# Second MLP in 128-token tiles that go by way of memory, with the inverse transform at a chunk's head and a new order of root, rows, bias row and transpositions

## The reference

```
h = layernorm(x, g1, be1)
h = afno2d(h, w1, b1, w2, b2)       # rfft2, block-diagonal filter, irfft2, + h
h = h + residual                     # called x3 here
m = layernorm(h, g2, be2)
m = gelu(m @ fc1_w + fc1_b) @ fc2_w + fc2_b
return m + h
```

## Time and profile before

| | us |
|---|---|
| median of 3 runs | 1118.7 (1117.19 to 1119.45) |
| profiled execution, own time | 1113.01 |
| its span (all times below count from its start) | 1111.2 |
| second MLP with its first inverse transform: 1012.56 to the end | 98.6 |
| second MLP, start of `up(0)` to the last matmul | 1022.53 to 1107.14 |

### The profile page before, as it was taken

One profiled execution on the slowest core, in us unless ns is written; L12 is line 12 of the kernel. 1 busy time (PEld: TensorE's weight loads), 2 busy tenths in 40 slices (PEclk: granted clock), 3 DMA queues, 4 the chain that ended last, 5 costly groups with the idle time before them and its releaser, 6 DMA issues.

```text
span 1111.2 us, 35967 instructions
## 1 busy us (share of the span) xinstructions
PE 1033.5 (93%) x15606; PEld 731.5 (66%) x15606; DVE 847.2 (76%) x1714; ACT 700.6 (63%) x1003; POOL 170.7 (15%) x142
## 2 busy tenths in 40 slices
PE   5867889999999999999999999999989889998998
PEld 3545246665777776677776767676657776775776
DVE  4837978889999999999999999999526764233443
ACT  4646157677787777777777877777865442231554
POOL 4430000910000000000000000000024544001443
PEclk9885579999999999999999999999999999999999
DMA  4698967657474756565656566554400001211110
GB/s 122 172 223 271 239 119 167 107 99 129 85 121 93 111 97 107 96 107 101 103 100 105 104 99 108 96 95 88 80 13 21 25 23 34 68 54 41 40 45 23
DMA packets 83011, 109.17 MB, mean 98 GB/s; under 512 B 14109, under 2 KB 75234, under 8 KB 82661
## 3 DMA queue, kind: packets, MB, share of 16 engines
q1 hardware_dynamic: 82853, 106.87, 48.9%
HBM read 85.40 MB, written 21.44 MB: 96 GB/s over the span
## 4 chain that ended last, share of the span: by engine, by line
PE 71%; DVE 12%; DMA 7%; ACT 5%; issue 3%; POOL 2%; SPq 0%; DVEq 0%; ACTq 0%; POOLq 0%
PE ps L1028 35%; PE ps L1189 17%; PE ps L1023 15%; DVE mx_p L1485 4%; DVE xh L101 2%; POOL rstd L109 1%; DMA m_d<-mneg 1%; DVE stage_lo L1454 1%; PE ps L1041 1%; ACT hid_f L955 1%; DVE stats L88 1%; DMA rel_d<-stage_lo 1%; DMA rel<-in_c_rel_w 1%; PE ps L1135 1%; DMA qv<-m_d 1%
## 5 line engine op out<-in xcount | busy, mean ns | idle before, releaser
L1485 DVE TENSOR_REDUCE mx_p<-ps 128x1 f32<-128x464 f32 (+1 forms) x1080 | 608.6, 629 | 34.4 <-PE ps L1028 23.2
L905 ACT ACTIVATE prob<-ps 128x768 f32<-128x768 f32 x648 | 496.2, 810 | 184.9 <-PE ps L1028 184.1
L1028 PE MATMUL ps<-kc,qc 112*32 112x464 f16 (+1 forms) x4320 | 460.4, 370 | 8.6 <-issue 4.4
L1028 PE MATMUL ps<-qv,ka 113*32 113x384 f16 x5184 | 403.8, 328 | 10.3 <-DMA qv<-m_d 7.7
L1189 PE MATMUL ps<-prob,v_ext 128*32 128x384 f32 x2592 | 293.3, 487 | 2.5 <-issue 2.0
L1028 PEld LDWEIGHTS ps<-qv,ka 113*32 113x32 f16 x5184 | 213.9, 97 | 86.7 <-issue 28.6
L1028 PEld LDWEIGHTS ps<-kc,qc 112*32 112x32 f16 x4320 | 173.2, 95 | 108.0 <-DVE mx_p L1485 30.0
L1189 PEld LDWEIGHTS ps<-prob,v_ext 128*32 128x32 f32 x2592 | 117.0, 111 | 17.4 <-issue 3.2
L1023 PE MATMUL ps<-w_dn,hid 128*96 128x192 f16 x864 | 77.5, 249 | 6.6 <-DVE hid L1540 4.4
L1023 PEld LDWEIGHTS ps<-w_dn,hid 128*96 128x96 f16 x864 | 73.2, 125 | 12.0 <-issue 6.1
L752 POOL COPY v_ext<-v_all 128x288 f32<-128x288 f32 x12 | 5.1, 427 | 480.6 <-PE ps L1189 480.5
(11 more groups left out here) (106 smaller groups left out, 838.2 us busy)
## 6 DMA issues: line engine op xcount, KB each, us to landing
qv<-rel_d SPq DMA_DIRECT2D x216, 144.0 KB
qv<-kq_d SPq DMA_DIRECT2D x108, 216.0 KB
qc<-rel_d SPq DMA_DIRECT2D x24, 216.0 KB, 4.0
xin<-in_x SPq DMA_DIRECT2D x12, 288.0 KB, 3.3
kq_d<-khl SPq DMA_DIRECT2D x24, 144.0 KB, 2.3
q_h<-kq_d SPq DMA_DIRECT2D x9, 288.0 KB, 4.7
q_w<-qw_d SPq DMA_DIRECT2D x9, 288.0 KB, 6.7
rel_d<-stage_hi SPq DMA_DIRECT2D x4, 648.0 KB, 7.6
```

What stands on the lines that cost most here:

```text
L905: nc.scalar.activation(prob[:, s4(p, s), :].rearrange("p (a b) -> p a b", a=2), ps[:, 3 + 2 * (s % 2):5 + 2 * (s % 2), 0:CW], ACT.Exp).the ...
L1028: ins = nc.tensor.matmul(ps[c:c + 32, bank, 0:w], l[:, c:c + 32], r, start=True, stop=True, tile_position=(0, c))
L1485: nc.vector.tensor_reduce(mx_p[:, q * GT + k // MP, k % MP:k % MP + 1], ps[:, slot, 0:min(MW, N - k % MP * MW)], AX, ALU.max).then_inc(uni ...
```

## The change

1. `down` of the second MLP works on 128-token tiles (W = 128): three tiles a chunk, 54 matmuls instead of 72, each with a stationary operand of 128 columns instead of 96.
2. The sum then needs x3 with 128 tokens on 128 partitions. SP writes x3 of a chunk to `x3_d` in memory and reads it back as `x3t` (128 x 3 x 192, two buffers); the sum (now two instructions) writes `y_o`, which is stored. `rows` is loaded on 128 partitions.
3. The row fc2_b is added to `x3t` by POOL (`bias_into_wide`, 576 elements a partition) at the head of a chunk; `bias_into` of x3 is gone from the second MLP.
4. PE does `inverse_w(c+1)` at the head of the chunk, ahead of `up(c)`, and the transpositions after the hi products of tiles 0 and 2 and ahead of their lo products.
5. POOL takes the root after hidden slices 0 and 1 and does slices 2 and 3 behind it. DVE does its hidden slices 4 and 5 behind the normalized rows, not beside the root, and the next input's lo part behind them.

```diff
+            def to_wide_tiles(c):
+                rows_c = x3_d[c * CW:(c + 1) * CW, :]
+                sp.wait_ge(x3_ok, c + 1)
+                sp.dma_start(rows_c.rearrange("(t p) c -> p t c", p=T), x1[:, ds(c * CT, CT), :]).then_inc(x3_out, 16)
+                sp.wait_ge(x3_out, 16 * (c + 1))
+                sp.dma_start(x3t[:, c % 2, :, :], rows_c.rearrange("(j p) c -> p j c", p=128))\
+                  .then_inc(x3t_in[c % 2], 16)
...
             def block1(c, more):
                 if more:
                     load_u2(c + 1)
                 if not is_at(c, 0):
                     store_out(c - 1)
+                if more:
+                    to_wide_tiles(c + 1)
 
             load_u2(0)
+            to_wide_tiles(0)
...
+            def bias_into_wide(c):
+                pool.wait_ge(x3t_in[c % 2], 16 * (c // 2 + 1))
+                x = x3t[:, c % 2, :, :]
+                nc.gpsimd.tensor_tensor(x, x, rows[:, 3:4, :].to_broadcast([128, 3, C]), ALU.add).then_inc(x3b_ok, 1)
+
             def block1(c, more):
-                lo_of_hidden(c, up1, range(POOL_TILES))
+                bias_into_wide(c)
+                lo_of_hidden(c, up1, range(2))
                 if more:
                     norm_root(pool, nc, rstd, ln4, c + 1)
-                    bias_into(c + 1, 3, ln4, x3b_ok)
+                lo_of_hidden(c, up1, range(2, POOL_TILES))
...
             def down(c, i, sems, half_way):
+                W, late = (T, (1, 3)) if i == 0 else (128, (1,))
...
+                if i == 1:
+                    half_way()
                 pe.wait_ge(sems["lo"], (c + 1) * HM)
                 for t in (0, 2):
                     lo_products(t)
-                half_way()
-                for t in (1, 3):
+                if i == 0:
+                    half_way()
+                for t in late:
...
             def block1(c, more):
-                up(c, 1, up1, {2: lambda: inverse_w(c + 1)} if more else {})
+                if more:
+                    inverse_w(c + 1)
+                up(c, 1, up1, {})
                 down(c, 1, up1, lambda: norm_transposed(c + 1, ln4, t4_ps) if more else None)
...
                 norm_chunk(dve, nc, x3_c, stats, mv, rstd, xh2[0], ln4, c,
                            lambda: wait_used(dve, t4_ps, c), beside_root)
-                lo_of_input(c, 1)
 
             def block1(c, more):
                 tiles = range(POOL_TILES, HM)
                 if more:
-                    inverse(c + 1, lambda: lo_of_hidden(c, up1, tiles))
-                else:
-                    lo_of_hidden(c, up1, tiles)
-                mlp_sum(c, up1, x3b_ok, lambda: wait_used(dve, y_out, 16 * c))
+                    inverse(c + 1, lambda: None)
+                lo_of_hidden(c, up1, tiles)
+                if more:
+                    lo_of_input(c + 1, 1)
+                dve.wait_ge(up1["dn_ps"], c + 1)
+                dve.wait_ge(x3b_ok, c + 1)
+                wait_used(dve, y_out, 16 * c)
...
+                nc.vector.scalar_tensor_tensor(out=y[:, 0:2 * C], in0=ps[:, 2, 0:2 * C], scalar=1 / WS,
+                                               in1=x3[:, 0:2 * C], op0=ALU.mult, op1=ALU.add)
+                nc.vector.scalar_tensor_tensor(out=y[:, 2 * C:3 * C], in0=ps[:, 3, 0:C], scalar=1 / WS,
+                                               in1=x3[:, 2 * C:3 * C], op0=ALU.mult, op1=ALU.add)\
+                  .then_inc(up1["sum"], 1)
```

More of the change, by code:

```diff
@@ L129, in build @@
         u1_d = nc.dram_tensor("u1_d", (S, 2, KF, C), F32).ap()
+        x3_d = nc.dram_tensor("x3_d", (N, C), F32).ap()
         u2_d = nc.dram_tensor("u2_d", (S, 2, KF, C), F32).ap()
@@ L134, in build @@
             khl = sb("khl", [C2, 2, 4, 2, CW], F16, r)
+        with ExitStack() as r:
+            x3t = sb("x3t", [128, 2, 3, C], F32, r)
+            y_o = sb("y_o", [128, 3, C], F32, r)
         attn = sb("attn", [T, NT, C])
@@ L143, in build @@
         shift = [sb(f"shift{i}", [C2, 2]) for i in range(3)]
-        rows = sb("rows", [T, 4, C])
+        rows = sb("rows", [128, 4, C])
         ident = sb("ident", [128, 128])
@@ L312, in build @@
         x3b_ok = sem("x3b_ok")
+        x3_out = sem("x3_out")
+        x3t_in = [sem("x3t_in0"), sem("x3t_in1")]
         ln4 = norm_sems("ln4")
@@ L319, in build @@
         x_t = d["x"].rearrange("(t p) c -> p t c", p=T)
-        out_t = out.rearrange("(t p) c -> p t c", p=T)
         NCONST = [0]
@@ L338, in load_weights @@
             for i, nm in enumerate(("L0_conv_mlp_b2", "L1_conv_g1", "L1_conv_be1", "L1_conv_fc2_b")):
-                load(eng, rows[:, i, :], d[nm].rearrange("(o c) -> o c", o=1).to_broadcast([T, C]))
+                load(eng, rows[:, i, :], d[nm].rearrange("(o c) -> o c", o=1).to_broadcast([128, C]))
         def load_transforms(eng):
@@ L695, in store_out @@
                 sp.wait_ge(up1["sum"], c + 1)
-                sp.dma_start(out_t[:, ds(c * CT, CT), :], y_sb[:, :, :]).then_inc(y_out, 16)
+                sp.dma_start(out[c * CW:(c + 1) * CW, :].rearrange("(j p) c -> p j c", p=128), y_o[:, :, :])\
+                  .then_inc(y_out, 16)
+            def to_wide_tiles(c):
[5 more added lines that the diff above has]
+                  .then_inc(x3t_in[c % 2], 16)
             def block1(c, more):
@@ L785, in bias_into @@
                 x1_c = x1[:, ds(c * CT, CT), :]
-                nc.gpsimd.tensor_tensor(x1_c, x1_c, rows[:, row:row + 1, :].to_broadcast([T, CT, C]),
+                nc.gpsimd.tensor_tensor(x1_c, x1_c, rows[0:T, row:row + 1, :].to_broadcast([T, CT, C]),
                                         ALU.add).then_inc(done, 1)
@@ L1277, in hi_products @@
                         for part in range(2):
-                            mm(down_tile(t), hid[:, m, 0, t * T:(t + 1) * T], w_dn[i][:, part, m, :],
+                            mm(down_tile(t), hid[:, m, 0, t * W:(t + 1) * W], w_dn[i][:, part, m, :],
                                start=(m == 0 and part == 0), stop=False)
@@ L1282, in lo_products @@
                     for m in range(HM):
-                        ins = mm(down_tile(t), hid[:, m, 1, t * T:(t + 1) * T], w_dn[i][:, 0, m, :],
+                        ins = mm(down_tile(t), hid[:, m, 1, t * W:(t + 1) * W], w_dn[i][:, 0, m, :],
                                  start=False, stop=(m == HM - 1))
@@ L1287, in down_tile @@
                 def down_tile(t):
-                    return ps[0:T, 2 + t // 2, (t % 2) * C:(t % 2 + 1) * C]
+                    return ps[0:W, 2 + t // 2, (t % 2) * C:(t % 2 + 1) * C]
                 wait_used(pe, sems["sum"], c)
@@ L1557, in block0 @@
                 nc.vector.tensor_tensor(h1[:, :, :], xh2[1][:, :, :],
-                                        rows[:, 1:2, :].to_broadcast([T, CT, C]), ALU.mult).then_inc(h1_mul, 1)
+                                        rows[0:T, 1:2, :].to_broadcast([T, CT, C]), ALU.mult).then_inc(h1_mul, 1)
                 dve.wait_ge(h1_mul, c + 1)
                 nc.vector.tensor_tensor(h1[:, :, :], h1[:, :, :],
-                                        rows[:, 2:3, :].to_broadcast([T, CT, C]), ALU.add).then_inc(h1_ok, 1)
+                                        rows[0:T, 2:3, :].to_broadcast([T, CT, C]), ALU.add).then_inc(h1_ok, 1)
             chunks(block0)
@@ L1596, in block1 @@
                 if more:
-                    inverse(c + 1, lambda: lo_of_hidden(c, up1, tiles))
-                else:
-                    lo_of_hidden(c, up1, tiles)
-                mlp_sum(c, up1, x3b_ok, lambda: wait_used(dve, y_out, 16 * c))
+                    inverse(c + 1, lambda: None)
[5 more added lines that the diff above has]
+                wait_used(dve, y_out, 16 * c)
+                x3 = x3t[:, c % 2, :, :].rearrange("p t c -> p (t c)")
+                y = y_o[:, :, :].rearrange("p t c -> p (t c)")
+                nc.vector.scalar_tensor_tensor(out=y[:, 0:2 * C], in0=ps[:, 2, 0:2 * C], scalar=1 / WS,
[3 more added lines that the diff above has]
+                  .then_inc(up1["sum"], 1)
             inverse(0, lambda: None)
+            lo_of_input(0, 1)
             chunks(block1)
```

1 line of the change is left out of this document (removed).

## The result

The changed kernel takes 1128.9 us (median of 4 runs, 1127.7 to 1132.8) against 1118.0 for the kernel before in the same comparison: ratio 1.012, 95% interval [1.0086, 1.0155]. That is 11 us slower, and outside the range of the prediction (1115.5 to 1123.1). The profiled execution took 1128.54 us with a span of 1126.8.

A forecast was written before the change was run, and what follows sets the result against it. PE was taken to bound a chunk, but for ACT's gelus. Five chunks at +0.61 (+3.05), last chunk -1.49, last sum -0.1 and chunk 0 -0.3 gave +1.2 us: 1119.9 us, 78%, range 1115.5 to 1123.1.

The forecast's parts named there:

- The pitch of the wide matmuls: PE in `down`: matmuls with 128-column stationary operands keep 82.5 ns each, so 18 fewer save 1.49 us a chunk.
- rival (c): PE in `down`: wide weight loads set the pitch, 98 ns, +3.2 us on top, 1123.1 us; chance 8%.
- The hole before slice 2: PE in `up`: without the inverse transform there, the wait for ACT's gelu of slice 0 is bare, +0.58 in five chunks.
- The last chunk: Second MLP's last chunk: no rows and no bias row, so the full saving of 1.49 us.
- rival (b): `x3t` lands only after 11.4 us of a chunk, so rows end at 10.4; chunk 13.9, 1114.6 us; chance 7%.
- rival (a): DVE and POOL don't hold each other up: rows end at 9.25 us, chunk 13.25, 1111.4 us; chance 7%.
- the bias row ends: POOL: bias row of the next chunk, 1.36 us behind hidden slices 2 and 3, ends 11.1 us into a chunk.
- The -0.3 at chunk 0's head: Chunk 0: the inverse transform may fill some of PE's 0.89 us idle; -0.3 us, bounds -0.9 and +1.0.
- Step 1: DVE's four rows beside POOL: one passes after each POOL instruction, the last goes free; rows end at 11.5 us.
- Step 2: PE before the transpositions: idle of 1.4 us a chunk, priced at its own length, with no clock term.
- the upper bound that the prediction gave it: Length of a chunk with a successor: 14.95 us forecast, bounds 14.9 and 15.4 for any `x3t` landing before 11.4.
- forecast +1.6: The six chunks of the second MLP: five at +0.61 us each and the last at -1.49.

The follow-up runs named there:

- the kernel with that edit alone: The kernel before, with only its inverse transform moved to the chunk's head: 1117.5 us, ratio 1.001.
- an experiment: The changed kernel without the norm's second wait ahead of DVE's rows (for PE's transpositions of the chunk before): 1125.0 us, one run.
- the tiles alone: Against the kernel before: wide tiles by way of memory, bias row at the chunk's start; inverse transform, root and transpositions in their old places: 1112.7 us, ratio 0.9958.
- the root first: The changed kernel with the bias row held until its own chunk has begun, and POOL's root ahead of all four hidden slices: 1113.1 us, ratio 0.9962.
- the last kernel: Changed kernel with late bias row, inverse transform before slice 2, POOL's slices 2 and 3 behind the rows, transpositions before the last hi products: 1114.1 us, ratio 0.9979.
- the first kernel of the experiments: The changed kernel with one wait that keeps POOL's bias row until the first slice of `up` of its chunk is done: 1115.4 us, ratio 0.9978.

## Why the prediction was wrong

**Right.** The pitch of the wide matmuls: 82.5 ns, rival (c) out. The hole before slice 2: +0.57 in the profile, +0.57 in the kernel with that edit alone. The last chunk: 11.41 against 12.91, -1.50. `x3t` lands before POOL wants it, rival (b) out. Rows meet the POOL series and the bias row is part of it, rival (a) out; the bias row ends 11.08 us after the chunk's start, where 11.1 was forecast. Every wait that the prediction lists shows up, with the releaser that it names. The -0.3 at chunk 0's head didn't come: PE waits 0.84 there for the spectrum's load, where it waited 0.89 for its input before.

**Step 1 that failed: "one row instruction gets through after each POOL instruction".** The rows end 12.07 us after the chunk's start (1072.65 - 1060.58) instead of 11.5: 0.99 behind the bias row and not 0.40, since three rows and not one are left when it ends. I read the passing rows off one chunk of the first MLP, the only one in that trace where rows run beside three POOL instructions without a gap, and took them for a rule. It is how long the first row lasts that varies: 3.20 here, 0.97 there, 1.84 in one chunk of an experiment. With the 82.5 ns matmuls that gives 15.55 a chunk, not 14.95: chunk 0 of the kernel after, and all of the kernel with filler matmuls. Five times 0.6: +3 us. On 1119.9 that is 1122.9, still inside the range; a chunk of 15.55 is 0.15 beyond the upper bound that the prediction gave it.

**Step 2, absent: TensorE's clock.** The prediction puts an idle of 1.4 us on PE in every chunk and prices it at its own length. It has no sentence on what the clock does behind it. Measured: 1.5 us more in each of four chunks, +6 us, the larger part of the miss. The kernel before held the warning in its own code: `stay_awake` fills PE's waits at the second MLP's start with matmuls that nobody reads. With PE's idle at 0.53 the clock didn't fall. The Trainium skill ("TensorE: Matmul & The Clock Gate", Part 1: The HAM clock gate) says that the gate follows how busy the engine was recently; the falls behind the longest wait of a chunk, and none with that wait filled, agree with it.

In sum, for the six chunks: forecast +1.6, hold +3, clock +6, together +10.6; the stretch shows +10.5 and the medians +11.0. The change had a gain in it: 4.1 us with the tiles alone, 2.9 with the root first. It was turned into a loss by one POOL instruction of 1.4 us placed where the rows wait.

## What to carry to other kernels

Price an instruction on GpSimd or VectorE by what the other of the two wants to start meanwhile: take the whole unbroken series as the bound, and count in both directions. Where a change adds an idle of TensorE to each turn of a loop, as the 1.9 us here, add a second term for the matmuls behind it at half clock (here 1.5 us a turn), as a range from none to all turns. And when work is taken off the busiest engine, name what it was hiding: here 1.49 us of matmuls came off and 0.6 arrived.

## What the runs showed of the hardware

- An elementwise instruction of VectorE can sit through three or four GpSimd instructions in a row (3.20 us; four slices in the kernel with the root first), and one of GpSimd through VectorE's (two slices in 2.50 instead of 1.79). Whether it slips in between varies from one chunk to the next in one execution. Not every meeting costs: in the second MLP before, POOL's root (1.02) and DVE's two hidden slices (1.03) run beside each other at their usual length.
- At equal idle (1.88 us) and equal work the clock fell in some chunks and not in others, and once behind 1.61; idles of 0.53, of 0.71, and of 1.1 to 1.4 us (the last kernel) brought none in the chunks of their profiles.
- The same code reaches the second MLP at different times. With equal programs up to there, chunk 0's head stands at 1028.01 in the changed kernel, and in the first kernel of the experiments at
```profile
1022.51 1.53 PE L1046 MATMUL ps<-u_sb,idft_w 100*96 100x384 f32 x4 [0.63 <-DMA u_sb<-u_d]
```
  Up to these heads the clock stood at 1.2 GHz for 102.4 us in the changed kernel's execution and for 92.2 in the other's; at half speed 10.2 us more are worth at most 5.1, an estimate that covers most of the 5.5 between them. Single runs of a kernel spread over some 10 us (30 runs of the kernel before: 1112.7 to 1122.0), so differences of a few us need many runs, or are read from the chunk lengths, which repeat to 0.1 us within a profile but for falls of the clock, for a row that passes earlier (0.18 less) and for one chunk of the last kernel (0.24 more).
